# A Perceiver block on one core: the head of the kernel is put in another order

## The reference

```
q = (layernorm(x) @ Wq.T + bq), k = (ctx @ Wk.T + bk), v = (ctx @ Wv.T + bv)   # 16 heads of 16
scores = q @ k.T / sqrt(16);  attn = softmax(scores);  out = (attn @ v) @ Wo.T + bo
```

## Time and profile before

| what | us |
|---|---|
| time, median of 3 runs | 701.08 (700.46 to 701.24) |
| the profiled execution: span from first to last instruction | 699.7 |
| TensorE busy in it | 671.0 |
| VectorE | 552.5 |
| ScalarE | 443.4 |
| GpSimd | 549.0 |

### The profile page before, as it was taken

How to read it: one execution, slowest core, us unless ns; L and a number is a source line. 1 busy time by engine, 2 the same in 40 slices (tenths; PEclk the granted TensorE clock), 3 DMA queues, 4 the chain that set the end, 5 groups by cost and what they waited for, 6 DMA issues and landing times.

```text
span 699.7 us, 21737 instructions
## 1 busy us (share of the span) xinstructions
PE 671.0 (96%) x8632; PEld 507.2 (72%) x8681; DVE 552.5 (79%) x1138; ACT 443.4 (63%) x885; POOL 549.0 (78%) x374
## 2 busy tenths in 40 slices
PE   4799999999999999999999999999999998899897
PEld 2556786877777877787778777877777786677673
DVE  4697877868888878778787868787868788888867
ACT  2446766666666666676767666767675787665830
POOL 7759999999699889798989789889788786723422
PEclk9999999999999999999999999999999999999999
DMA  8587055454445454545353645363543450000212
GB/s 309 143 213 214 27 138 162 99 155 97 150 113 155 105 164 92 160 107 165 93 165 84 178 102 159 85 187 89 169 97 104 100 164 4 2 2 9 91 69 91
DMA packets 45610, 84.20 MB, mean 120 GB/s; under 512 B 8668, under 2 KB 28420, under 8 KB 45508
## 3 DMA queue, kind: packets, MB, share of 16 engines
q1 hardware_dynamic: 43896, 80.13, 41.9%
q0 software_dynamic: 912, 2.14, 1.0%
q10 hardware_dynamic: 704, 0.55, 0.3%
HBM read 36.89 MB, written 6.55 MB: 62 GB/s over the span
## 4 chain that ended last, share of the span: by engine, by line
PE 82%; DVE 5%; DMA 5%; SPq 2%; issue 2%; POOL 2%; ACT 2%; ACTq 0%; DVEq 0%; POOLq 0%
PE ps_kv L821 17%; PE ps_kv L812 16%; PE ps_score L872 12%; PE ps_out L896 12%; PE ps_front L844 12%; PE ps_score L920 2%; SPq L502 2%; DMA kstack<-khigh 2%; PE ps_out L912 1%; DMA cbuf<-in_ctxT 1%; PE ps_kv L783 1%; DMA wq_sb<-in_wqT 1%; PE ps_front L920 1%; PE ps_front L853 1%; PE ps_kv L920 1%
## 5 line engine op out<-in xcount | busy, mean ns | idle before, releaser
L637 POOL TENSOR_TENSOR plow<-prob 128x1024 bf16<-128x1024 f32 (+1 forms) x198 | 372.1, 1898 | 58.8 <-ACT prob L1242 56.3
L1511 DVE TENSOR_REDUCE maxes<-ps_front 128x1 f32<-128x512 f32 (+1 forms) x416 | 267.1, 666 | 57.2 <-PE ps_front L844 53.9
L1242 ACT ACTIVATE prob<-ps_score 128x512 f32<-128x512 f32 (+1 forms) x416 | 236.2, 598 | 71.0 <-PE ps_score L872 61.9
L872 PE MATMUL ps_score<-qstack,kstack 98*128 98x128 bf16 (+1 forms) x1664 | 150.5, 219 | 0.8 <-ACT prob L1242 0.5
L844 PE MATMUL ps_front<-kstack,qstack 96*128 96x512 bf16 (+1 forms) x512 | 145.4, 333 | 2.7 <-DMA kstack<-khigh 1.9
L872 PEld LDWEIGHTS ps_score<-qstack,kstack 98*128 98x128 bf16 (+1 forms) x1664 | 112.1, 98 | 33.7 <-ACT prob L1242 1.9
L896 PE MATMUL ps_out<-vstack,prob 128*128 128x65 bf16 (+1 forms) x1664 | 113.6, 194 | 0.7 <-POOL plow L637 0.3
L821 PE MATMUL ps_kv<-w_hi,cbuf 128*128 128x256 bf16 (+1 forms) x402 | 109.7, 273 | 0.9 <-DVE vstack L1501 0.9
L1494 DVE SCALAR_TENSOR_TENSOR klow<-ps_kv,bcol,khigh 128x512 bf16<-128x512 f32 (+1 forms) x123 | 76.8, 629 | 42.5 <-ACT khigh L1220 42.0
L821 PE MATMUL ps_kv<-w_hi,clow 128*128 128x256 bf16 (+1 forms) x402 | 109.5, 272 | 0.0
L821 PE MATMUL ps_kv<-w_lo,cbuf 128*128 128x256 bf16 (+1 forms) x402 | 109.5, 272 | 0.0
(11 more groups left out here) (290 smaller groups left out, 858.7 us busy)
## 6 DMA issues: line engine op xcount, KB each, us to landing
kstack<-khigh SPq DMA_DIRECT2D x256, 100.1 KB, 2.2
cbuf<-in_ctxT SPq DMA_DIRECT2D x15, 1601.0 KB, 7.2
kstack<-klow SPq DMA_DIRECT2D x128, 100.1 KB, 2.2
qstack<-q_blocks SPq DMA_DIRECT2D x48, 64.0 KB, 2.3
q_blocks<-qbd SPq DMA_DIRECT2D x16, 128.0 KB, 2.0
cbuf<-in_weT SPq DMA_DIRECT2D x2, 1024.0 KB, 7.8
slot_x<-att_all SPq DMA_DIRECT2D x8, 128.0 KB, 7.1
vstack<-slot_x SPq DMA_DIRECT2D x4, 256.0 KB, 3.6
```

The costliest lines, as they stand in the source:

```text
L637: nc.gpsimd.tensor_tensor(plow[slot][0:n, :], prob[slot][0:n, :], p_high(slot, 0, HP * P)[0:n], ALU.subtract).then_inc(plow_gps, 1)
L872: mm = nc.tensor.matmul(ps_score[0:nn, h % NSB, j * P:(j + 1) * P], kstack[par][0:98, hp, n0:n0 + nn], qstack[par][0:98, q_at(hp), :], sta ...
L1242: nc.scalar.activation(prob[slot][0:nn, e * 512:e * 512 + 512], ps_score[0:nn, h % NSB, :], ACT.Exp)\
L1511: nc.vector.reduce_max(maxes[:, hp:hp + len(unit), n], ps[:, 0:len(unit) * nn].rearrange("p (h k) -> p h k", k=nn), AX.X).then_inc(m_free, 1)
```

## The change

`FIRST_ORDER` has unit 7 directly behind 6, and unit 17 only before 13. The four strings are rewritten over their first 40 to 200 letters, with the same letters in sum (GpSimd's has two c fewer, see below). On TensorE the first maximum comes after unit 9 instead of after unit 10; the maxima then come in groups of two, three and five with a unit between; behind maximum 14 seven units come in a row: 17, 13, 18, 14, and units 0, 1 and 2 of batch 1. On VectorE the value weights' parts (B) come before the first `klow`; the variance (z) of tile 1 comes behind maximum 5, and its query rows (j) between maxima 12 and 13. On ScalarE the first query copy (g) comes ahead of the first key unit. GpSimd's string was `qcvccvvfqcfvvcvcvfcc` and then the probabilities; it becomes `vcvvcfqvvfvcccqvc`, five of the probabilities, `f`, and the others. In that string v is a value unit's low part, c a context quarter, q a tile's normalisation, and f a step of the second stage's weights.

The loads: SyncE no longer loads seven tiles of x in its fixed part; ScalarE loads tile 1 and SyncE the other six, behind the first four head pairs of batch 0. GpSimd's wqkv and wg loads move into its first f. Its first two quarters of batch 1's `clow` move from the string into the fixed part, ahead of the eight small loads.

Tile 0's rows are normalised on VectorE. TensorE begins with 56 products of constant ones into a bank of scores that isn't used yet, and has 34 more ahead of the first query product.

```
-FIRST_ORDER = [15, 16, 0, 1, 2, 3, 4, 5, 17, 6, 8, 9, 10, 11, 12, 7, 13, 18, 14]
+FIRST_ORDER = [15, 16, 0, 1, 2, 3, 4, 5, 6, 7, 8, 9, 10, 11, 12, 17, 13, 18, 14]
...
 PE_PROGRAM = [
-    ("KKKKKKKKKKKKKmmKmmKmKmKmmKmKmKmmKmKmmmKKmmKmKmmKmKmmKKmmKmKmmsKmsmsKmsmsKmwsmswmwsKsmswmwwmKmsswmKwm"
+    ("KKKKKKKKKKKKmmKmmmmmKmmmKmmmmmKKKKKKKmmmKKmKmKmmKKmmmKKmmKsKmmKmmssKmsmsKssmmKmswwswmsmKswmKmswwsmww"
...
-    ("KKgKKKKKKKKKKKKKKgKKKKKKKKKKKKRKKReKeeeeKeKeeKeeKeeeeeeKKeeeeeeKeeReeKReeeKeKeeKeeKeeKeKeeKeKeeeegeeK"
+    ("KgKKKKKKKKKKKKKKKgKKKKKKKKKKKKRKeKRKeeKeeeKeeKeeeKeeKeeeKeeeeeeKeeRKeeReeeKeKeeKeeKeKeeeKeKeKeeeegeeK"
...
-    ("jKKKkKBzKkzKKCKmmmmmkmKmmjmmKmKmmKmKzmmKmKmmKmKmmKKmmKmKmKmKmmKmmmKmKmmmmKmKmmmmmKmmKmmmmmKmmKvKmmKm"
+    ("jKBKKKKKKkKCmmmmKmmzmmmkmmmmjmKmKKmKzKmmKmmKKmmKmKmmKKmKkmKmmKKmmmmKmmmKzmmKmmmmmKKmmmmmmmKmmkKvKmmK"
...
-    ("qcvccvvfqcfvvcvcvfccppppppppppppppppppccppcpcppppcpqppppfcpppcppcppppccpcppfpcpppppppppcppppppcppcpc"
+    ("vcvvcfqvvfvcccqvcpppppfppppppppppppccpppcpcppppcpqppppfcpppcppcppppccpcppfpcpppppppppcppppppcppcpcpp"
...
-            sp.dma_start(x_all[:, D:TILES * D].rearrange("p (t d) -> p t d", t=TILES - 1),
-                         x.rearrange("(t p) d -> p t d", p=P)[:, 1:TILES, :]).then_inc(ld_x2, 16)
...
+            def load_queries(b):
+                sp.wait_ge(q_sent, 32 * (b // 2 + 1))
+                for g, n in enumerate((0, 0, 1)):
+                    sp.dma_start(qstack[b % 2][32 * g:32 * g + 32, :, :].rearrange("p (r o) c -> p r (o c)", o=KT),
+                                 q_dram[n, b].rearrange("(r p) n -> p r n", p=32)).then_inc(q_loaded, 16)
...
             def keys(b):
-                sp.wait_ge(q_sent, 32 * (b // 2 + 1))
-                for g, n in enumerate((0, 0, 1)):
-                    sp.dma_start(qstack[par][32 * g:32 * g + 32, :, :].rearrange("p (r o) c -> p r (o c)", o=KT),
-                                 q_dram[n, b].rearrange("(r p) n -> p r n", p=32)).then_inc(q_loaded, 16)
+                if b:
+                    load_queries(b)
                 for t in range(KT):
                     wait_free(sp, [(b, u) for u in range(NPIECE * t, NPIECE * (t + 1))])
                     for r in range(4):
...
+                        if b == 0 and t == 0 and r == 0:
+                            load_queries(0)
+                    if b == 0 and t == 0:
+                        sp.dma_start(x_all[:, 2 * D:TILES * D].rearrange("p (t d) -> p t d", t=TILES - 2),
+                                     x.rearrange("(t p) d -> p t d", p=P)[:, 2:TILES, :]).then_inc(ld_x2, 16)
...
             def query_norm(t):
                 pool.wait_ge(var0_rdy, t + 1)
                 nc.gpsimd.tensor_tensor(rs0[:, :], ve0[:, :], half_neg[:, 0:1], ALU.pow).then_inc(rs0_rdy, 1)
+                if t == 0:
+                    return
                 pool.wait_ge(rs0_rdy, t + 1)
-                if t:
-                    pool.wait_ge(kv_done, KV_AT[query_unit(t - 1, NREAL)] + 1)
+                pool.wait_ge(h0_rdy, t)
+                pool.wait_ge(kv_done, KV_AT[query_unit(t - 1, NREAL)] + 1)
...
+            for quarter in range(2):
+                low_context(1, quarter)
...
-            pool.dma_start(wqkv_sb[:, :, :], wqkv.rearrange("(k p) n -> p k n", p=P)).then_inc(ld_t, 16)
-            pool.dma_start(wg_sb[:, :, :], wg.rearrange("(k p) n -> p k n", p=P)).then_inc(ld_t, 16)
...
                 if n == 0:
+                    pool.dma_start(wqkv_sb[:, :, :], wqkv.rearrange("(k p) n -> p k n", p=P)).then_inc(ld_t, 16)
+                    pool.dma_start(wg_sb[:, :, :], wg.rearrange("(k p) n -> p k n", p=P)).then_inc(ld_t, 16)
...
+            def warm(products):
+                for _ in range(products):
+                    nc.tensor.matmul(ps_score[:, 0, 0:P], ones_bf[:, :], ones_bf[:, :], start=True, stop=True)
+
+            pe.wait_ge(ones_set, 1)
+            warm(56)
...
                 if query_tile(b, u) == 0:
+                    warm(34)
                     pe.wait_ge(ld_wq, 16)
...
+            act.dma_start(x_all[:, D:2 * D], x[P:2 * P, :]).then_inc(ld_x1, 16)
...
+            dve.wait_ge(rs0_rdy, 1)
+            nc.vector.tensor_scalar(h0[:, :], x_all[:, 0:D], mv0[:, 0:1], rs0[:, :], ALU.subtract, ALU.mult)\
+                .then_inc(h0_rdy, 1)
             weight_parts(0)
...
             dve.wait_ge(ld_b, 16)
-            nc.vector.tensor_scalar_mul(bq4[:, :], bcol[:, 0, :], DH ** -0.5).then_inc(bq4_rdy, 1)
-            dve.wait_ge(ld_c, 16)
-            nc.vector.tensor_copy(ident_bf[:, :], ident)
...
-                    q = nc.vector.tensor_scalar(cols, cols, DH ** -0.5, bq4[:, o:o + 1], ALU.mult, ALU.add)
+                    q = nc.vector.tensor_scalar(cols, cols, bcol[:, 0, o:o + 1], DH ** -0.5, ALU.add, ALU.mult)
...
             def second_part_constants():
+                dve.wait_ge(ld_c, 16)
+                nc.vector.tensor_copy(ident_bf[:, :], ident)
```

More of the change, by code:

```diff
@@ L110 @@
 PE_PROGRAM = [
-    ("KKKKKKKKKKKKKmmKmmKmKmKmmKmKmKmmKmKmmmKKmmKmKmmKmKmmKKmmKmKmmsKmsmsKmsmsKmwsmswmwsKsmswmwwmKmsswmKwm"
-     "wssmKsmswmwswmsmKsmsmwwsmswmwsmsKmwmsswmKmwwwswswwwswsKmmsswwmKsmswwKmssmKwwmssmwwmKmmsKmmswKmmssKwm"
+    ("KKKKKKKKKKKKmmKmmmmmKmmmKmmmmmKKKKKKKmmmKKmKmKmmKKmmmKKmmKsKmmKmmssKmsmsKssmmKmswwswmsmKswmKmswwsmww"
+     "wmssmKmswmswwsmmKswsmmwswsmwmswsmKmmwsswmKwmwswwswswwsKmsmKswmsmwswKwmsmKmwswmsmKssmmKwsmmwKmssmwwKm"
      "swsmwwmswsKmsmwKmsKmsswmwmKmsswwKmwwwmKwsmKsKmswsmwwsmsKmmssKwmwsmswwmKswmwmwwssKmsmKmwswmmsKmsswwmm"
@@ L129 @@
 ACT_PROGRAM = [
-    ("KKgKKKKKKKKKKKKKKgKKKKKKKKKKKKRKKReKeeeeKeKeeKeeKeeeeeeKKeeeeeeKeeReeKReeeKeKeeKeeKeeKeKeeKeKeeeegeK"
+    ("KgKKKKKKKKKKKKKKKgKKKKKKKKKKKKRKeKRKeeKeeeKeeKeeeKeeKeeeKeeeeeeKeeRKeeReeeKeKeeKeeKeKeeeKeKeKeeeegeK"
      "eKeeeKeKKeeRKRKeeeeKeeKeeKeKeeeKeeeKeeKeeKeeeKKeeKReKeKRKeeeKeKeeeKeKeeKKeeeKeKeeKeeKeeeegeeKeKeRKKR"
@@ L140 @@
 DVE_PROGRAM = [
-    ("jKKKkKBzKkzKKCKmmmmmkmKmmjmmKmKmmKmKzmmKmKmmKmKmmKKmmKmKmKmKmmKmmmKmKmmmmKmKmmmmmKmmKmmmmmKmmKvKmmKm"
-     "mkmKmmKmmmmKmKmmmKmjmmKKmmKmmammKmKKmKKmmmKvmKmmmmKKmmmmKmmKmmmmKmKmKmmKmmmKmKKaKmmKmmKvmmKmKmmKmzKm"
+    ("jKBKKKKKKkKCmmmmKmmzmmmkmmmmjmKmKKmKzKmmKmmKKmmKmKmmKKmKkmKmmKKmmmmKmmmKzmmKmmmmmKKmmmmmmmKmmkKvKmmK"
+     "mmKmmmKmmmmKmKmmmKmjmmKKmmKmmammKmKKmKKmmmKvmKmmmmKKmmmmKmmKmmmmKmKmKmmKmmmKmKKaKmmKmmKvmmKmKmmKmzKm"
      "KmmmmKmammkjmmKmmKmKmmKmKKKvKKmmKmmmKmmmKKmmmKmmmmKmammKmmKmKmmKmmKmKKvKKmKmmmKmmKmmKzkmmaKmmmKmmKmK"
@@ L151 @@
 POOL_PROGRAM = [
-    ("qcvccvvfqcfvvcvcvfccppppppppppppppppppccppcpcppppcpqppppfcpppcppcppppccpcppfpcpppppppppcppppppcppcpc"
-     "ppppqcpppcpppccpppppppcpppppcpcppcpppppqcppppppccppcpppppccppppppcpppcppppqcppppppppppcccpppppppppcc"
-     "pcpcppppqpppppppcppcpccppppcpppcppcpppcpppppcppppppppccpcpppppppppppppppppbbpprrtZbptrbIbtbIIbrRrRbt"
-     "tRrrRtrsRsIsttssRRYYRggggYg", 1),
+    ("vcvvcfqvvfvcccqvcpppppfppppppppppppccpppcpcppppcpqppppfcpppcppcppppccpcppfpcpppppppppcppppppcppcpcpp"
+     "ppqcpppcpppccpppppppcpppppcpcppcpppppqcppppppccppcpppppccppppppcpppcppppqcppppppppppcccpppppppppccpc"
+     "pcppppqpppppppcppcpccppppcpppcppcpppcpppppcppppppppccpcpppppppppppppppppbbpprrtZbptrbIbtbIIbrRrRbttR"
+     "rrRtrsRsIsttssRRYYRggggYg", 1),
 ]
@@ L266, in build @@
         bvcol = sb("bvcol", [P, 2, KT])
-        bq4 = sb("bq4", [P, KT])
         wq_sb = sb("wq_sb", [P, KT, D])
@@ L387, in build @@
         ld_ones, ld_ones2, qbd_hi_rdy, q_rdy = (sem(n) for n in ("ld_ones", "ld_ones2", "qbd_hi_rdy", "q_rdy"))
-        ld_x, ld_x2, ld_c, ld_wk, ld_wv, ld_wq, ld_b, ld_t, ld_o, ld_row, ld_e = (
-            sem("ld_" + n) for n in ("x", "x2", "c", "wk", "wv", "wq", "b", "t", "o", "row", "e"))
-        ones_set, st0_rdy, mv0_rdy, var0_rdy, rs0_rdy, bq4_rdy = (
-            sem(n) for n in ("ones_set", "st0_rdy", "mv0_rdy", "var0_rdy", "rs0_rdy", "bq4_rdy"))
+        ld_x, ld_x1, ld_x2, ld_c, ld_wk, ld_wv, ld_wq, ld_b, ld_t, ld_o, ld_row, ld_e = (
+            sem("ld_" + n) for n in ("x", "x1", "x2", "c", "wk", "wv", "wq", "b", "t", "o", "row", "e"))
+        ones_set, st0_rdy, mv0_rdy, var0_rdy, rs0_rdy = (
+            sem(n) for n in ("ones_set", "st0_rdy", "mv0_rdy", "var0_rdy", "rs0_rdy"))
         fills_set = sem("fills_set")
@@ L719, in low_experts @@
                 nc.gpsimd.tensor_tensor(we_low[k][:, a:a + 4 * D], w, high(w), ALU.subtract).then_inc(we_rdy, 1)
-            contexts = iter([(b, quarter) for b in BATCHES[1:] for quarter in range(4)])
+            contexts = iter([(b, quarter) for b in BATCHES[1:] for quarter in range(4)][2:])
             chunks, folds, roots = iter(GPS_LOW), iter(range(3 + KT)), iter(range(1, TILES))
-            contexts_done, values_done, chunks_done, norms_done, values = 3, 0, 0, 1, iter(range(KUNITS, NREAL))
+            contexts_done, values_done, chunks_done, norms_done, values = 5, 0, 0, 1, iter(range(KUNITS, NREAL))
             tiles = {kind: iter(range(TILES)) for kind in "btrRI"}
@@ L1394, in query_moments @@
             def query_moments(t):
```

(5 more changed lines are left out.)

## The result

The changed kernel takes 707.5 us (median of 4 executions, 705.79 to 708.99) against 700.93 for the kernel before (700.46 to 701.24, 4 executions): ratio 1.0087, 95% interval 1.0073 to 1.0101. It is slower by 6.1 us by the ratio (6.6 between the medians), where 2.8 us faster was forecast. The profiled execution's span grew from 699.7 to 704.6 us.

What follows compares the result with a forecast made beforehand. TensorE's work in written order bounds the body; 14.5 us idle lie before 65 us. At maximum 25 TensorE is 2.9 us earlier, VectorE 2.8: span 699.7 becomes 696.9, plus 1.4 around it 698.3; range 695.4 to 701.0.

Steps and rivals of the forecast that it cites:

- The body is TensorE's work in order: From 100 to 200 us TensorE is busy 99.19 of 100 us; reaching the body earlier moves the end as much.
- the constant products raise the clock: TensorE's head: clock up by 9.4 us, queries end at 10.5, unit 0 at 11.9 instead of 13.85.
- GpSimd's chain to unit 17: Part 4, GpSimd's queue, the step let decide: unit 17's rows at 34.0 us, so TensorE idles 2.0 us.
- the second context: Load of batch 1's context: lands at 15.1 us instead of 17.1, without 0.77 MB ahead of it.
- The shared port: VectorE's normalisation beside GpSimd's context work could lose 1.5 us: rows at 7.8, the sum not moved.
- part 3: SyncE's queue: first maximum at 22.5 us instead of 29.16; rest of x takes 2 us, pair 4 at 31.
- the sum's stretch from unit 17 to maximum 25: TensorE from unit 17 at 34.1 us: to 37.4, then 16.3 us more, to 53.7.
- the head's forecast of -2.9: TensorE's work up to maximum 25 ends at 53.7 us instead of 56.6, 2.9 earlier.
- later stretches: Body after the head: idle 0.8 us in 100 us before, the same after.
- a body whose idle time grew: Sign that the forecast is wrong: it would show the end not following the head.
- D: Rival: collisions stretch GpSimd's chain to unit 17, rows at 38.6 us, 1.7 slower, 702.8 us; chance 0.07.
- A: Main case: TensorE idles 2.0 us for GpSimd's rows ahead of unit 17, 698.3 us; chance 0.48.

Runs made afterwards that it cites:

- e3: The changed kernel without its 90 constant products; ratio 1.0070 against the kernel before.
- e1: The changed kernel with VectorE's statistics of tile 2 moved behind the query rows; ratio 1.0063 against the kernel before.
- e16: e15 with the loads of wqkv and wg moved to the end of GpSimd's second f; ratio 1.0004 against the kernel before.
- e2: The changed kernel with the rest of x loaded where it was before, ahead of batch 1's context; ratio 1.0096 against the kernel before.
- e4: The kernel before with only the 90 constant products added; ratio 1.0013 against the kernel before.
- e7: The changed kernel with the rest of x behind pair 7's rows and tile 2's statistics behind the fourth key unit, 90 products; ratio 1.0060 against the kernel before.
- e10: e9 with 90 constant products instead of 128; ratio 1.0049 against the kernel before.
- e13: The changed kernel as it is, a second trace; one execution, 706.17 us.
- e5: The kernel before with 128 constant products added; ratio 0.9999 against the kernel before.
- e6: The changed kernel with 128 constant products instead of 90; ratio 1.0070 against the kernel before.
- e8: e7 with 128 constant products instead of 90; ratio 1.0020 against the kernel before.
- e9: e8 with GpSimd's rows of tile 1 ahead of the fold that issues the wqkv and wg loads; ratio 1.0003 against the kernel before.
- e11: e9 with the rest of x issued behind pair 3's rows again; ratio 1.0021 against the kernel before.
- e12: e11 with the loads of wqkv and wg at the end of GpSimd's second f; ratio 1.0042 against the kernel before.
- e14: e6 again, a second trace; one execution, 706.51 us.
- e15: e9 with VectorE's statistics of tile 2 moved right before the letter that uses them; ratio 1.0001 against the kernel before.

## Why the prediction was wrong

**Right.** The body is TensorE's work in order, and up to about 29 us the steps came as computed: the constant products raise the clock (in the traces they are worth 2.1 us at the first maximum and 2.7 at maximum 25, e3 against the change), the first key product at the high level, first maximum, issue of x. GpSimd's chain to unit 17 ended at 35.2 against 34.0; 0.9 of the difference is the second context, 16.0 instead of 15.1.

**The shared port.** The normalisation on VectorE, priced at 0.4 us, took 1.72, starting 0.05 ahead of a GpSimd instruction. By the lock of which the Trainium skill tells (SBUF — State Buffer, section SBUF: two separate sides) the prediction had estimated that it could lose 1.5 us; it took 1.3 over its price, which fits in size. The section also gives the ports to the engine that starts first, and by the trace that was VectorE; on that point the trace doesn't agree. What the step takes with GpSimd idle no trace shows. As the prediction said, it did not move the sum: wqT and the query products came when they would have.

**The step that failed first: part 3, "the rest of x, 0.8 MB ... 2 us at 385 GB/s, pair 4 at 31".** It took 6.3 us in the change and 5.3 to 7.5 us in the 13 other traces that load it in the loop, some 105 to 150 GB/s, shared with key rows and in part with wqkv. I used the mean rate of many queues at once for one load in rows of 1 KB; the load of the same shape in the kernel before, seven tiles issued at 3.16 us, took 10.0 us. And I priced the transfer without asking who waits for it: the kernel shows the wait (`dve.wait_ge((ld_x, ld_x1, ld_x2)[t], 16)`, at t = 2) and the program its place, 'k' between maxima 8 and 9. e1 takes exactly that out and gives back 1.6 us in the trace and, with intervals that overlap, 0.0024 of the ratio (1.7 us).

**The second: the sum's stretch from unit 17 to maximum 25, 19.6 us of TensorE work with no wait in it.** It was 23.1 us (35.63 to 58.73). In e16, without either fault and at the full clock, it was still 22.0: 19.9 busy, and 2.1 idle, nearly all of it short waits (0.65 for the query blocks' low parts, two of 0.57 for maxima, 0.2 for a klow) of the kind that stand in the trace of before as well. e16, TensorE's stretch:

```profile
33.48:55.50 22.02, 19.89 (x140) 12.22 (x140) 15.99 (x32) 9.88 (x19) 17.92 (x19) 1.00 0.84 247
```

The rest of the 23.1 is the low clock: TensorE is busy for 20.98. So the head's forecast of -2.9 missed by 5.0: 1.5 for the late arrival, 2.1 idle, 1.1 for the clock, and 0.3 of rounding and of the work itself. Even the mended change had some 1.5 us to gain, not 2.9.

**The third: "later stretches: idle 0.8 in 100 us before, the same after".** 3.0 us were lost between 325 and 417 us. No rival had this; only the last sign of being wrong, "a body whose idle time grew", named it. Constant products were costed by the time that they fill, not by the instructions that they add. Every trace with 90 lost 1.0 to 3.3 us there (after, e1, e2, e4, e7, e10, e13), no trace with 0 or 128 did (e3; e5, e6, e8, e9, e11, e12, e14; the products of e15 and e16 are 128 too). That window flatters 128: from 75 us to the last maximum the seven traces with 90 lost 0.7 to 4.1 us, and of the ten others e3, e8, e9, e12 and e15 lost 1.1 to 1.7, mostly at other places. That the count is the cause is shown, by the traces and by e7 with e8 and e9 with e10 in the timed runs; that the way leads through slow issues on SyncE rests on coincidence in the traces (27 of 28), since no run takes a code load away by itself.

**Rivals.** D (slower, by GpSimd's chain) had the sign and not the mechanism; its place did decide e2 and e8. A's wait at unit 17 was absent only because TensorE was late itself.

**What stays open.** Of 6.1 us, e1 gives back 1.7 and e6 1.2 when each is undone alone (by the ratios' middles; their intervals touch the change's), and both with the later x, rows and loads (e15, e16) 5.8 to 6.0. Taken one after the other the steps add up: the wait for x, with x itself later (e7, 1.0060), gives back 1.9, the count of products (e8, 1.0020) 2.8, GpSimd's rows first (e9, 1.0003) 1.2, the statistics last (e15, 1.0001) 0.1; each ratio has an interval of about 1 us either way. So a fault gives back less while another stands. How much of each step is the fall of the clock, and how much a wait that differs from execution to execution, isn't settled.
